# Four graph layers on one core: statistics split in layer 0, channel steps spread over five units, f1 and the third norm earlier on the way into layer 3

## What is computed

```python
h = jnp.maximum(_layernorm(x), 0.0); x = x + L0(h)   # GAT, elu
h = jnp.maximum(_layernorm(x), 0.0); x = x + L1(h)   # softmax per channel
h = jnp.maximum(_layernorm(x), 0.0); x = x + L2(h)   # 4 dot-product heads, out unit, layernorm
h = jnp.maximum(_layernorm(x), 0.0); x = x + L3(h)   # GAT, relu
# L0 and L3:
e = leaky_relu(s1[:, :, None] + s2[:, None, :], 0.2) + mask
h_prime = softmax(e, axis=2) @ Wh      # then elu (L0) or relu (L3)
# L1:
feat = softplus(x * (INV_SQRT2 * w0) + b0); scores = feat * wa + ba
out = einsum('bijd,bjd->bid', softmax_j(scores masked), feat)
```

## Time and profile before

| | us |
|---|---|
| median of 3 runs | 2041.74 (2040.82 to 2042.96) |
| the profiled execution's own time | 2039.39 |
| its span, first to last instruction | 2037.6 |
| PE busy | 1908.2 (94%) |
| DVE busy | 1685.1 (83%) |
| ACT busy | 1245.3 (61%) |
| POOL busy | 1037.3 (51%) |

### The profile page before, as it was taken

One profiled execution on the slowest core, in us unless ns is written; L12 is line 12 of the kernel. 1 busy time (PEld: TensorE's weight loads), 2 busy tenths in 40 slices (PEclk: granted clock), 3 DMA queues, 4 the chain that ended last, 5 costly groups with the idle time before them and its releaser, 6 DMA issues.

```text
span 2037.6 us, 94849 instructions
## 1 busy us (share of the span) xinstructions
PE 1908.2 (94%) x43528; PEld 1566.7 (77%) x43528; DVE 1685.1 (83%) x2005; ACT 1245.3 (61%) x1860; POOL 1037.3 (51%) x738
## 2 busy tenths in 40 slices
PE   5888779999999999999999999999999999989998
PEld 4777679987777777777777777777777777767787
DVE  5888878868778888888888888888888888867998
ACT  4877545426666666666666666666666666644342
POOL 6566678723235445454454554545545445354653
PEclk8999889999999999999999999999999999999999
DMA  6000000001111111111111111111111111101111
GB/s 178 4 4 3 3 2 3 2 12 34 34 34 34 34 34 30 37 31 33 35 30 37 31 33 35 30 36 32 34 34 34 34 34 34 34 13 24 24 25 34
DMA packets 88254, 61.22 MB, mean 30 GB/s; under 512 B 45616, under 2 KB 86832, under 8 KB 87856
## 3 DMA queue, kind: packets, MB, share of 16 engines
q1 hardware_dynamic: 85632, 54.57, 10.9%
q10 hardware_dynamic: 2224, 0.59, 0.1%
HBM read 8.98 MB, written 4.19 MB: 6 GB/s over the span
## 4 chain that ended last, share of the span: by engine, by line
PE 67%; DVE 13%; ACT 7%; POOL 7%; issue 2%; DMA 1%; SPq 1%; POOLq 0%; ACTq 0%; DVEq 0%
PE ACC L1547 29%; PE S L1727 23%; PE S L1706 5%; DVE ring L1326 4%; PE AX L1770 3%; DVE ring L1194 2%; PE AX L1779 2%; PE AX L1747 2%; POOL sp_log L759 1%; POOL ln_sq L762 1%; ACT st_x L871 1%; ACT ring L1000 1%; PE AX L1527 1%; DVE ch_rden L1311 1%; ACT st_x L867 1%
## 5 line engine op out<-in xcount | busy, mean ns | idle before, releaser
L1547 PEld LDWEIGHTS ACC<-V,ring 128*64 128x64 f32 x28672 | 961.9, 139 | 202.4 <-DVE ring L1194 52.2
L1326 DVE TENSOR_TENSOR ring<-ring,mask_self_t 128x1024 f32<-128x1024 f32 x640 | 892.5, 1404 | 194.3 <-ACT ring L1000 189.8
L1547 PE MATMUL ACC<-V,ring 128*64 128x65 f32 x28672 | 981.2, 224 | 51.3 <-DVE ring L1194 32.5
L1000 ACT ACTIVATE ring<-S,dot_bias 128x1024 f32<-128x1024 f32 x640 | 713.3, 1115 | 409.5 <-PE S L1727 372.9
L1727 PE MATMUL S<-FA 128*64 128x512 f16 x5120 | 666.0, 382 | 1.8 <-DMA FA<-lo 1.5
L1727 PEld LDWEIGHTS S<-FA 128*64 128x64 f16 x5120 | 253.6, 110 | 161.5 <-ACT ring L1000 15.8
L1194 DVE SCALAR_TENSOR_TENSOR ring<-S,pair_q,mask_t 128x1024 f32<-128x1024 f32 x256 | 314.7, 1273 | 20.9 <-ACT S L914 5.0
L775 POOL TENSOR_TENSOR EV_both<-score,recip 128x512 f32<-128x512 f32 x64 | 124.3, 1942 | 315.5 <-DVE score L1335 315.4
L1706 PE MATMUL S<-parts,mask_t 128*128 128x128 bf16 x3072 | 176.1, 220 | 14.0 <-DVE X L1315 13.8
L1706 PEld LDWEIGHTS S<-parts,mask_t 128*128 128x128 bf16 x3072 | 174.3, 99 | 15.6 <-issue 15.5
L768 POOL TENSOR_TENSOR V<-v_pairs,bh_bc 128x512 f32<-128x512 f32 x64 | 96.5, 1507 | 118.2 <-ACT v_pairs L1020 118.2
(11 more groups left out here) (126 smaller groups left out, 1993.2 us busy)
## 6 DMA issues: line engine op xcount, KB each, us to landing
FA<-hi SPq DMA_DIRECT2D x320, 64.0 KB, 2.1
FA<-lo SPq DMA_DIRECT2D x320, 64.0 KB, 2.0
X<-in_x SPq DMA_DIRECT2D x16, 256.0 KB, 4.9
ring<-in_adj SPq DMA_DIRECT2D x8, 512.0 KB, 8.0
out_x<-X SPq DMA_DIRECT2D x16, 256.0 KB, 2.6
wh<-in_wh_t ACTq DMA_DIRECT2D x2, 64.0 KB, 6.4
bh_bc<-in_bh ACTq DMA_DIRECT2D x1, 128.0 KB, 9.3
w_gat<-in_w_gat ACTq DMA_DIRECT2D x4, 16.0 KB, 4.0
```

Of the source, the lines that this page charges most:

```text
L1000: act.activation(ring[:, jt, :], S[jt % 2][:, :], ACT.Exp, bias=dot_bias[:, n % 2:n % 2 + 1])\
L1326: dve.tensor_tensor(ring[:, jt, :], ring[:, jt, :], mask_self_t[:, jt, :], ALU.mult)\
L1547: last = pe.matmul(acc_of(t)[rows, :], ring[:, jt, t * P + c * CUT:t * P + (c + 1) * CUT], values, start=(jt == 0 and t % 4 == 0), stop=(j ...
```

## The change

1. In layer 0 `late_norm_sums` is split. Its eight means (`late_shifts`) stand ahead of `gat_factors`, its squared sums (`late_squares`) stay behind `gat_below`. The lower half of the elu is clamped by GpSimd right behind `gat_divide` (min(o, 0), in layer 0 only), and ScalarE only takes exp. `gat_elu` moves from behind tile 6 to behind tile 7.
2. Steps -5 to -1 of layer 1 stand one to a unit, in units 11 to 15. On VectorE each is cut into four parts, behind tiles 1, 3, 5 and 6; on GpSimd each stands ahead of `gat_add`; on ScalarE at the end of the unit. Norms of layer 1 use two halves of `z_t`.
3. At the way into layer 3: f1 of graphs 0 and 2 goes ahead of one tile's sums on TensorE. GpSimd does the norm of graph 2 and the node values of graph 0 ahead of `out_scale`. The values, features and bound of `LAST` move one tile ahead on TensorE, its norms and bias one tile ahead on VectorE, and `stat_var` behind the bias.

```diff
+        ch_xc, ch_y = z_t[:, 0, 0:TD], z_t[:, 0, TD:2 * TD]
...
-        STEPS_BESIDE = {(B - 2, 1): -5, (B - 2, 4): -4, (B - 2, 7): -3, (B - 1, 2): -2, (B - 1, 5): -1}
+        AHEAD = 5
...
-            return [STEPS_BESIDE[cur, jt] for jt in range(T) if (cur, jt) in STEPS_BESIDE]
+            return [cur - B] if cur >= B - AHEAD else []
...
             def gat_divide(layer, b):
...
                 pool.tensor_tensor(tiles(o[:, :]), accs[:, :, 1:D + 1], cols(recip[:, :]), ALU.mult).then_inc(gat_o, 1)
+                if layer == 0:
+                    wait(pool, elu_made, b)
+                    pool.wait_ge(gat_o, n + 1)
+                    pool.tensor_scalar(below[:, :], o[:, :], 0.0, None, ALU.min).then_inc(elu_below, 1)
...
-                    for k in steps[:2]:
+                    for k in steps:
                         channel_step(k, k % 2)
                     if cur > 0:
                         gat_add(layer, cur - 1)
-                    for k in steps[2:]:
-                        channel_step(k, k % 2)
...
                 node_biases(3, 0)
+                gat_norm(3, 2)
+                node_values(3, 0)
                 out_scale(B - 2)
-                node_values(3, 0)
                 stat_rstd(3, B - 3)
-                gat_norm(3, 2)
...
             def gat_below(b):
-                act.wait_ge(gat_o, b + 1)
-                act.activation(below[:, :], o[:, :], ACT.Relu, scale=-1.0).then_inc(elu_below, 1)
                 act.wait_ge(elu_below, b + 1)
-                act.activation(below[:, :], below[:, :], ACT.Exp, scale=-1.0).then_inc(elu_exp, 1)
+                act.activation(below[:, :], below[:, :], ACT.Exp).then_inc(elu_exp, 1)
...
                         h_relu(layer, cur + 2)
+                    if late_stats(layer, cur) is not None:
+                        late_shifts(late_stats(layer, cur))
                     if cur + 1 < B:
                         gat_factors(layer, cur + 1)
...
-                        late_norm_sums(late_stats(layer, cur))
+                        late_squares(late_stats(layer, cur))
...
-                        if jt == 6 and cur > 0 and layer == 0:
+                        if jt == 7 and cur > 0 and layer == 0:
                             gat_elu(cur - 1)
-                        if layer == 0 and (cur, jt) in STEPS_BESIDE:
-                            channel_step(STEPS_BESIDE[cur, jt], STEPS_BESIDE[cur, jt] % 2)
+                        if layer == 0 and jt in (1, 3, 5, 6):
+                            for k in steps_beside(cur):
+                                channel_part(k, k % 2, (1, 3, 5, 6).index(jt))
...
-                    if jt == 4:
+                    if jt == 3:
                         norms(LAST)
                     if jt == 5:
                         feature_rest(LAST)
                     if jt == 6:
+                        bias(LAST)
+                    if jt == 7:
                         stat_var(3, B - 2)
-                    if jt == 7:
-                        bias(LAST)
...
-                    if jt == 1:
+                    if jt == 0:
                         values(LAST)
-                    if jt == 3:
+                    if jt == 2:
                         features(LAST)
-                    if jt == 5:
+                    if jt == 4:
                         spread_bound(LAST)
...
                     if jt < T:
                         dots(m)
+                    if jt == T - 1:
+                        gat_gain(3, FIRST)
                     if jt >= LAG:
                         dot_sums(m - LAG)
...
                     if m < end:
                         dots(m)
+                    if m == end:
+                        gat_gain(3, 0)
                     if m >= LAG:
                         dot_sums(m - LAG)
```

More of the change, by code:

```diff
@@ L575, in ln_center @@
                 wait(pool, ln_pool, 4 * n)
-                if n == 0:
+                if layer == 2 and b == 0:
                     pool.wait_ge(y_made, 2 * B)
                 pool.wait_ge(ln_dve, 4 * n + 2)
-                pool.tensor_tensor(tiles(ln_xc[:, :]), x_of(b), cols(ln_mean[:, :]), ALU.subtract).then_inc(ln_pool, 1)
+                xc = ch_xc if layer == 1 else ln_xc[:, :]
+                pool.tensor_tensor(tiles(xc), x_of(b), cols(ln_mean[:, :]), ALU.subtract).then_inc(ln_pool, 1)
                 if layer == 2:
@@ L589, in ln_scale @@
                 pool.wait_ge(ln_pool, 4 * n + 3)
-                y = tiles(ln_y[:, :]) if layer == 1 else ln_y[:, :].rearrange("p (q h d) -> p h q d", q=T // 2, h=2)
+                y = tiles(ch_y) if layer == 1 else ln_y[:, :].rearrange("p (q h d) -> p h q d", q=T // 2, h=2)
                 by_half = (lambda ap: ap) if layer == 1 else halves_of
-                pool.tensor_tensor(y, by_half(tiles(ln_xc[:, :])), by_half(cols(ln_rstd[:, :])), ALU.mult)\
+                xc = ch_xc if layer == 1 else ln_xc[:, :]
+                pool.tensor_tensor(y, by_half(tiles(xc)), by_half(cols(ln_rstd[:, :])), ALU.mult)\
                     .then_inc(ln_pool, 1)
@@ L751, in first_norm @@
                 ln_center(2, 0)
-                pool.wait_ge(ch_zt, B)
+                y_is_read(AX_AT["T", 0, B - 1])
                 ln_scale(2, 0)
@@ L857, in gat_sums, with late_shifts @@
                 copy_acc(ACT.Relu if layer == 3 else ACT.Copy)
-            def late_norm_sums(b):
+            def late_shifts(b):
                 par, n = b % 2, b - EARLY
@@ L868, in late_norm_sums, with late_squares @@
                                    accum_out=st_shift[:, par, t:t + 1]).then_inc(late_shifted, 1)
+            def late_squares(b):
+                par, n = b % 2, b - EARLY
                 act.wait_ge(late_shifted, T * (n + 1))
@@ L1282, in channel_step, with channel_part @@
             def channel_step(k, par):
+                for part in range(4):
+                    channel_part(k, par, part)
+                channel_result(k, par)
+            def channel_part(k, par, part):
                 b = k + 4
-                if exists(b):
+                if exists(b) and part == 0:
                     ln_var_of(1, b)
                 b = k + 1
-                if exists(b):
+                if exists(b) and part == 1:
                     dve.wait_ge(ch_p1, b + 1)
@@ L1292, in channel_step @@
                 b = k + 5
-                if exists(b):
+                if exists(b) and part == 1:
                     ln_mean_of(1, b)
                 b = k + 3
-                if exists(b):
+                if exists(b) and part == 2:
                     dve.wait_ge(ch_log, b + 1)
@@ L1301, in channel_step @@
                 b = k + 1
-                if exists(b):
+                if exists(b) and part == 3:
                     dve.wait_ge(ch_p2, b + 1)
@@ L1305, in channel_step, with channel_result @@
                         .then_inc(ch_p3, 1)
+            def channel_result(k, par):
                 b = k - 1
@@ L1830, in dot_layer @@
                             gat_columns(3, 0)
-                    if m == end:
-                        gat_gain(3, 0)
                     if m == end + 1:
```

8 lines of the change are left out of this document (2 added, 6 removed).

## The result

| | before | after |
|---|---|---|
| median of 16 runs each, us | 2042.55 | 2034.12 |
| lowest to highest | 2040.19 to 2046.65 | 2030.02 to 2037.71 |
| ratio, 95% interval | | 0.9958 [0.995, 0.9966] |
| profiled execution, its span | 2039.39, 2037.6 | 2037.51, 2035.7 |

The change makes the kernel 8.4 us (0.4%) faster. The sign is as forecast; 21.3 us had been forecast, with a range that ended at 12. The profiled execution of after is among its longest, so of the two traces I compare passages and not the ends: from the last weights of layer 0 to the end of layer 2 it took 4.9 us longer.

The account below looks back on a forecast made before the run. Bound: a loop across ScalarE and GpSimd in layer 0, with no engine full. Gains of 14.6, 1.2 and 5.7 less 0.25 made 21.3 us, taking the median from 2041.7 to 2020.4; range 2011 to 2030.

Parts of the forecast that it names:

- The loop of ScalarE and GpSimd: Layer 0's regular units: each engine waits for the other, setting the 13.89 us pace; 12.13 forecast after the change.
- Part 1: Layer 0's loop: means and relu leave it, GpSimd's clamp enters; 14.6 us faster, between 11.5 and 17.
- The first term of the loop: Layer 0: from the small exponentials to the elu's exp, 3.45 us with a clamp of 0.75.
- The floor of VectorE: Layer 0: VectorE needs 12.02 us a unit, nearly tying with the other loop, so 12.25 was taken.
- The elu's move: Layer 0: putting the elu behind tile 7 costs nothing, as GpSimd's sum into x comes far behind it.
- Part 2: Layer 1's steps, one to a unit in units 11 to 15: 1.2 us faster, between 5 slower and 7 faster.
- the 42.5: Units 11 to 13: forecast total in us with one step to a unit, against 35.1 before.
- Part 3: The way into layer 3: earlier norm, f1 and LAST's work give 5.7 us, between 3 and 6.5.
- the cover that I had named: Way into layer 3: biases and BEFORE's division come by 1831 and 1832, needed by 1833 to 1834.
- The steps hold up twice as much: Rival on units from 11 on: more waits and slower GpSimd, steps cost 5, time 2026.6 us; chance 0.15.
- Slower: Rival on layer 0: a clamp of 3.5 us in the loop makes the whole 7 slower, 2049 us; chance 0.04.
- the marks that I had given: Signs in the trace: distances near 12.2, clamp 0.55 to 1.07, little elu wait, last weights 12 to 22 us earlier.

Follow-up runs that it names:

- split_only: The kernel before with only the eight means moved ahead of the value copy; 2029.38 us, ratio 0.9923.
- rstd_next: After with relu back on ScalarE, steps at their old places, and GpSimd's root of the late statistic in the next unit; 2012.97 us, ratio 0.9847.
- feat_late: After with the last two parts of each step's features put behind tile 7 in layer 0; 2030.45 us, ratio 0.9928.
- square_behind: After with relu on ScalarE, root in the next unit, late features, and step squares behind the next copy of the sums; 2012.98 us, ratio 0.9856.
- part3_look: Before with only the way into layer 3 changed, run for its trace; the same kernel measured 2036.01 us, ratio 0.9967.
- relu_on_act: After with GpSimd's clamp taken back and relu on ScalarE again; 2019.67 us, ratio 0.9882.
- relu_steps_old: After with relu back on ScalarE and the five steps at their old places; 2015.33 us, ratio 0.9869.
- mix_late: After with relu on ScalarE, the root in the next unit, and steps one to a unit with late features; 2013.40 us, ratio 0.985.
- norm_late: After with GpSimd's third norm and node values of layer 3 back behind out_scale; 2040.13 us, ratio 0.9983.

## Why the prediction was right or wrong

**What bounds the kernel: right.** The loop of ScalarE and GpSimd set the pace. With the clamp as measured, its sum is 12.87, and a unit took 12.86; the step from 13.89 to 12.05 by the means alone (split_only) shows that they were in it. Below about 12 this loop is not the only bound: in rstd_next its wait was gone, and the distance fell only from 11.85 to 11.55.

**Part 1: the mechanism right, one term mis-sized.** The step that failed is "Its ends are the copy's rate, [...] so about 0.55, and the two-input division at 1.07. I take 0.75, nearer to the copy, since it too reads one input". The copy's end was right for a copy (0.61). But the clamp computes, and a one-input minimum on this tile takes 1.49, longer than the two-input division (1.07), which I had taken for the upper end. Fewer inputs was no reason for a lower bound on time, and nothing in the trace said so; "no row shows a one-input operation" should have left the upper end at least at the longest simple operation on that tile, the sum into x at 1.27, and a factor above it. The Trainium skill ("GPSIMD Engine Reference", section "Elementwise — side-by-side cycle accounting") has 768 ns for 512 elements in its best loop, and 2.6 cycles an element for two inputs; here two inputs took 1.04 us, and one input with arithmetic 1.49. The same page, section "Engine selection", calls one-input operations "roughly line-rate", which the copy bears out and the minimum does not; the measurement decides. The first term of the loop was 4.18 instead of 3.45, and a unit 12.86 instead of 12.25: 8 x 0.61 = 4.9 of the 6.1 that part 1 missed. Another 0.9 is unit 0, which took 0.7 longer than in before where 0.2 less was forecast. With the relu left on ScalarE the same part gives distances of 11.85: the clamp, meant to unload ScalarE, took back half of what the moved means gave.

**The floor of VectorE: too high.** "It needed 215.88 - 203.86 = 12.02 us" was a period, not its work: it held an elu of 1.20 instead of 0.69 and 0.67 us of idle time. Kernels ran at 11.85 and 11.55, and single units without late statistics at 10.5 to 11.5. The elu's move, which I had said costs nothing, gave 0.2 a unit. I had made that floor a reason to round the loop up, so this error hid behind the first. The elu took 0.71 or 0.86 in some units and 1.38 to 1.55 in others. This fits what the Trainium skill says in "GPSIMD Engine Reference", section "Specifications", on two inputs from SBUF, but a longer elu didn't go with a longer unit in rstd_next.

**Part 2: the wrong sign.** From the exponentials of unit 11 to the last weights the trace of after is 5.7 us slower, where 1.2 faster was forecast (and 5 slower was my bound). Against the old places in an otherwise equal kernel, the new ones cost 6.4 us of layer 0 with the clamp on GpSimd and 4.4 without it, so the sign was wrong even apart from the clamp. The mechanisms were the ones named: the square ahead of the sums' copy waited 2.79 and 5.44 us, the logarithm 4.41 and 3.15. Unit 11 was forecast at 13.8 and took 14.7, unit 12 13.5 and 14.9, unit 13 15.2 and 16.9; the rest 28.5 and 31.4. So the 42.5 that I had summed for units 11 to 13 was 46.6. Two causes of the sizes can be read from the traces: each unit holds the clamp's extra 0.74, and the waits feed each other (unit 13's logarithm stands behind exp, which stands behind the clamp). TensorE, waiting, also fell to the lower clock (1.93 for f1), which my sum had at nothing: by the stage tables the granted clock was 0.86 from 190 to 227 us, where before had 1.00 from 188 to 224. That this cost time isn't shown: feat_late had 0.82 in the same stretch and a layer 0 that was 6.0 shorter. The squares, which I had as the first cost, were no net loss where they were moved (square_behind, with relu on ScalarE); the logarithm was (feat_late).

**Part 3: nearly right.** 4.1 for norm and f1 (4.7 forecast), 0.8 for f1 of graph 2 (0.6). Of the cover that I had named, the need was mis-set, not the supply: the biases come at 1832.7 in after, where this passage stands 2.1 us later, so at 1830.6 by before's times, and 1831 was forecast. But ScalarE was ready for them at 1831.4 (1829.3 by before's times), not at 1833, and waits 1.54. What that wait cost isn't shown. For `LAST`, 0.4 gain became 0.9 loss: one hi issue held SyncE's queue for 1.68 us. The other traces bear this out: with a longest issue of 0.85, 1.29, 1.68 and 1.85 us the passage from the sums' copy to the first dots takes 29.2, 29.6, 30.0 and 30.2 (square_behind, part3_look, relu_on_act, rstd_next).

**The rivals.** None was it. "The steps hold up twice as much" priced part 2 at 5 slower, close to the 5.7 of the trace, but missed part 1. "Slower" had the right cause, the clamp in the loop, at prices (2.4 and more) above the true 1.49. The case that came is a clamp of 1.5 together with a loss in part 2, and I had priced each rival alone.

Of the marks that I had given, three told at once: a clamp of 1.49 outside 0.55 to 1.07, a wait of 0.98 ahead of the elu, and last weights only 2.7 us earlier, where less than 12 was to mean wrong. The fourth was set too wide: distances of 12.9 are not near 12.2, yet only above 13 was to mean wrong.

## What to carry to other kernels

Before work is moved to another engine, count the term that it adds to the loop and not only the one it takes away; and where no row shows the operation's form, put the upper end above every simple operation on that tile, however few its inputs. Moving the eight means alone was worth 15.7 us; with the relu left where it was and the steps too, the change gives 27 (relu_steps_old), and with the root a unit later 31 (rstd_next, 0.9847 [0.9832, 0.9862]), not clear of the 27; mix_late and square_behind are its equals. Of work put beside others' tiles, ask how many tiles lie between a result and its reader: two tiles more were worth 6 us of layer 0.

## What the runs showed of the hardware

- GpSimd, 128x512 f32 in SBUF: copy 0.61 us; product or minimum with a constant 1.49 to 1.51; product of two tiles 1.04. For 256 elements the minimum took 0.85, so some 2.5 ns an element and 0.2 fixed.
- TensorE, for the same eight products of f1: 1.04 us at the granted clock of 1.00 (2.4 GHz) and 1.93 at the lower level (0.50, 1.2 GHz), in norm_late after a wait of 4.14 us. With that gap the passage was 6 us longer.
- In after, in part3_look and in eight more kernels with the new way into layer 3, one of `LAST`'s eight issues on SyncE took 1.3 to 1.85 us instead of about 0.60 (in square_behind 0.85); in before and split_only none did. In after it was the third of the eight; what it waits for isn't shown.
